# A graph kernel on one core: the mask product of its one-hot gather in float32r instead of bf16

## The chip, the cores and the metric

The kernel runs on one core of one Trainium2 chip. The metric is the device time of one execution in microseconds (us). TensorE is the matrix engine, with weight loads and matmuls as instructions of their own; VectorE, ScalarE and GpSimd are the other engines, and the queue that starts plain transfers is called SP. In the profile they are PE and PEld (the loads), DVE, ACT, POOL and SP.

## The reference

There are 12500 nodes with 16 features and 412500 edges, sorted by their destination. Three edge-conditioned convolutions are followed by a layer that takes a maximum over edges.

```python
def _nnconv(x, src, dst, edge_attr, ew, eb, rw, rb):
    W = (edge_attr @ ew + eb).reshape(edge_attr.shape[0], x.shape[1], rw.shape[1])
    xj = x[src]
    msg = jnp.einsum('ei,eio->eo', xj, W)
    agg = jax.ops.segment_sum(msg, dst, num_segments=x.shape[0])
    return agg + x @ rw + rb
...
# the last layer
msg = inputs[src] * timestamp
h = jax.ops.segment_max(msg, dst, num_segments=inputs.shape[0])
return h @ W.T + b
```

Each of the four layers therefore needs the rows `x[src]` of all its edges: a gather of 412500 rows.

## The kernel before

**The chunks.** The edges lie as 128 streams, one on each partition, and a stream is cut into 124 chunks of 26 edges. `edges` (L556) runs over the chunks in each of the four layers, two chunks in a loop body, with two buffers of everything (slots 0 and 1). Of a chunk's 26 columns, 16 (`TG`) are fetched by GpSimd with one indirect DMA each (`pool_gather`, L461), from a table in memory. The other 10 (`TP`) are gathered by TensorE.

**TensorE's gather.** One step (`pe_step`, L619) fetches 128 rows. A node number is split in three: a lane (128), a zone (4) and a block in the zone (25, `NEAR`). The stationary operand `hot_key` is a one-hot matrix of the lanes, one for each zone; the moving operand is one zone of the node table, 25 blocks of 16 features, so 400 columns. The table is held in two float32r parts that add up to the float32 value, so 4 zones times 2 parts make eight products, accumulated in one PSUM bank. They leave the features of all 25 blocks. A ninth product, over 25 rows, adds to every block but the right one a large negative number: `not_near` is a huge number times the distance of the edge's block number from each of the 25, and `near_mask` is minus the unit matrix, each entry repeated 16 times. VectorE then takes the maximum over the 25 blocks (`pick`, L741), which gives the 16 features. There are four such banks; a step waits until the pick of four steps earlier has freed its bank (`s_pick`), and a pick waits for the ninth product (`s_gath`). Products take one weight load and one matmul each.

**ScalarE** makes the one-hot matrices out of keys that SP loads: `apart` (L508), `hot_key` (L513) and, last for a chunk, `not_near` (L524), each of 1280 columns for a chunk's 10 steps.

**The order in a chunk.** TensorE's order is written out in `pe_body` (L657): steps 4 to 6 of a chunk, a transpose of the first five picked rows (`pe_turn`, L637), steps 7 and 8, the product of those with the edge weights (`pe_product`, L649), step 9, then steps 0 to 3 (`HEAD`) of the following chunk with the second transpose and product among them. VectorE's order in `body` (L747) is: picks 4 and 5 of the next chunk; the product of the gathered rows with the edge attributes; pick 6; the same product for TensorE's rows; pick 7; the sum over features (L804); pick 8; the indices for the chunk after the next (L845), on which GpSimd waits; the second sum; pick 9; then picks 0 to 3 of the chunk after that, with 16 scans (L828) between them. In the max layer there are no transposes and no products by TensorE, and the indices follow pick 6.

**Start and layers.** All inputs are loaded once by SP, `near_mask` among them (L203); `vector_masks` (L247) prepares masks and keys on VectorE before the first layer. `parts_of_h` (L881 to 883) writes the table's two parts before each layer. Between layers lie batch norms, small products and a gather of each node's last edge.

Of the kernel before, what the change touches and what calls it, by code (L numbers as in the profile page):

```python
# [5 lines left out]
F32, BF16, F16, I32 = mybir.dt.float32, mybir.dt.bfloat16, mybir.dt.float16, mybir.dt.int32  # L6
F32R = mybir.dt.float32r
# [5 lines left out]
N, D, EF, E, LAYERS = 12500, 16, 8, 412500, 3  # L13
# [18 lines left out]
NEAR = 25  # L32
# [4 lines left out]
PE_EDGES = TP * P  # L37
# [14 lines left out]
def build(nc, io):  # L52
    ctx = ExitStack()

    def sb(name, shape, dt=F32):
        return ctx.enter_context(nc.sbuf_tensor(name, shape, dt))
# [4 lines left out]
    def slots(make, name, *a):  # L61
        return [make(f"{name}{s}", *a) for s in range(SLOTS)]

    with ctx:
# [37 lines left out]
        edge_i = sb("edge_i", [P, 4], I32)  # L102
# [19 lines left out]

        parts = [sb(f"part{k}", [P, ZONES * NEAR, D], F32R) for k in range(2)]
        zone_lane = sb("zone_lane", [P, ZONES + 1])
        near_mask = sb("near_mask", [NEAR, NEAR, D], BF16)
        keys = slots(sb, "keys", [P, PE_EDGES], F16)
        nears = slots(sb, "nears", [P, PE_EDGES], F16)
        apart = slots(sb, "apart", [P, PE_EDGES], F16)
        hot_key = slots(sb, "hot_key", [P, ZONES, PE_EDGES], F32R)
        not_near = slots(sb, "not_near", [NEAR, PE_EDGES], BF16)  # L130
        xe = slots(sb, "xe", [P, TP * D])
        xeT = sb("xeT", [TH * D, P])

# [60 lines left out]
        def bump(s, n=1):  # L194
# [5 lines left out]
                       (ident, io["ident"]), (conv_w, io["conv_w"][0])]  # L200
        loads = [(pe_src, io["pe_src"]), (src, io["src"]), (lanes, io["lanes"]),
                 (real, io["real"]), (lin_w, io["lin_w"]), (gamma, io["gamma"]), (beta, io["beta"]),
                 (edge_i, io["borders"]), (zone_lane, io["zone_lane"]), (near_mask, io["near_mask"]),  # L203
                 (row_i, io["borders_row"]), (edge_w, io["edge_w"][0])]

        def sync_start(e):
# [8 lines left out]
        def step(e, ins):  # L215

            ins.then_inc(s_step.sem, 1)
            s_step.n += 1
            e.wait_ge(s_step.sem, s_step.n)

        def tt(e, out, a, b, op):
            return e.tensor_tensor(out, a, b, op)  # L222
# [23 lines left out]

        def vector_masks(e):  # L247
            e.wait_ge(s_in.sem, IN_ALL)
            first, last, prev_last, next_first = (edge_i[:, k:k + 1] for k in range(4))
            tt(e, edge_m[:, 0:1], first, prev_last, ALU.is_equal)  # L250
            tt(e, edge_m[:, 1:2], first, last, ALU.is_equal)
            step(e, tt(e, edge_m[:, 2:3], next_first, last, ALU.is_equal))

            step(e, tt(e, edge_m[:, 3:4], edge_m[:, 1:2], edge_m[:, 2:3], ALU.mult))
            step(e, e.tensor_scalar(edge_m[:, 4:5], edge_m[:, 3:4], -1.0, 1.0, ALU.mult, ALU.add))
            e.tensor_scalar(head_lo_i[:, 0:1], first, P - 1, None, ALU.bitwise_and)
            step(e, e.tensor_scalar(head_lo_i[:, 1:2], first, 7, None, ALU.logical_shift_right))
            step(e, e.tensor_copy(edge_m[:, 0:2], head_lo_i[:, 0:2]))
            step(e, e.tensor_scalar(head_lo[:, :], lanes[:, :], edge_m[:, 0:1], edge_m[:, 4:5],
                                    ALU.is_equal, ALU.mult))  # L260
            step(e, e.tensor_scalar(head_hi[:, :], lanes[:, 0:NB], edge_m[:, 1:2], None, ALU.is_equal))

            rf, rpl, rpf = (row_i[:, k, :] for k in range(3))
            tt(e, row_m[:, 0, :], rf, rpl, ALU.is_equal)
            step(e, tt(e, row_m[:, 1, :], rpf, rpl, ALU.is_equal))
            step(e, tt(e, row_m[:, 2, :], row_m[:, 0, :], row_m[:, 1, :], ALU.mult))

            e.tensor_scalar(row_m[:, 3, :], row_m[:, 0, :], BIG, -BIG, ALU.mult, ALU.add)
            step(e, e.tensor_scalar(row_m[:, 4, :], row_m[:, 2, :], BIG, -BIG, ALU.mult, ALU.add))

            step(e, e.tensor_scalar(zone_f, pe_src, float(NEAR * P), None, ALU.is_ge))
            for z in range(2, ZONES):
                step(e, e.scalar_tensor_tensor(zone_f, pe_src, float(z * NEAR * P), zone_f, ALU.is_ge, ALU.add))

            step(e, e.scalar_tensor_tensor(pe_tmp, zone_f, -float(NEAR * P), pe_src, ALU.mult, ALU.add))
            step(e, e.tensor_scalar(pe_tmp, pe_tmp, 7, None, ALU.logical_shift_right))
            step(e, e.tensor_copy(keys[1][0:CHUNKS, :], pe_tmp))

            step(e, e.tensor_scalar(pe_src, pe_src, P - 1, None, ALU.bitwise_and))
            e.scalar_tensor_tensor(keys[0][0:CHUNKS, :], zone_f, float(P), pe_src, ALU.mult,  # L280
                                   ALU.add).then_inc(s_v.sem, 1)
# [3 lines left out]
        def masks_and_keys():  # L285

            on("vector")(vector_masks)
            v = bump(s_v)

            def sync_keys(e):  # L290
                e.wait_ge(s_v.sem, v)
                for ap, half in ((key_rows, keys[0]), (near_rows, keys[1])):
                    e.dma_start(ap, half[0:CHUNKS, :]).then_inc(s_keys.sem, 16)
                e.wait_ge(s_keys.sem, 32)
            on("sync")(sync_keys)
# [1001 lines left out]
```

## Time and profile before

| what | us |
|---|---|
| median of 3 runs | 17138.0 (17130.03 to 17155.55) |
| the profiled execution, its own time | 17104.02 |
| span in its profile | 17102.1 |
| TensorE matmuls busy | 12418.0 |
| GpSimd busy | 8073.4 |
| VectorE busy | 7231.8 |
| ScalarE busy | 6262.2 |

The span runs from the first to the last instruction. The mean granted clock of TensorE was 0.81 of its full 2.4 GHz; it is granted at full or at half. The first three layers take the most time; the last begins after about 13000 us. Busy times are sums over stretches of very different kinds, and a matmul's end is modelled by the profiler, so a busy TensorE need not be the bound.

### The profile page before, as it was taken

What the parts mean: (1) busy time and instruction counts of PE and PEld (TensorE: products, weight loads), DVE (VectorE), ACT (ScalarE), POOL (GpSimd) and SP (SyncE); (2) the same over time, 40 slices, a digit from 0 to 9 for tenths busy, and PEclk for the clock granted to TensorE, in tenths of its full rate; (3) what the DMA queues carried; (4) which work ended last, traced back from release to release, by engine and by line L of the source; (5) the groups of instructions that cost most, each with busy time, mean ns of one, the idle gap of its engine ahead of it and who ended that gap; (6) DMA issues with size and microseconds to landing.
All of it is one profiled execution on the core that took longest, in us unless ns stands there. A gap on an engine that the chain in (4) does not pass through costs nothing.

```text
span 17102.1 us, 173153 instructions
## 1 busy us (share of the span) xinstructions
PE 12418.0 (73%) x48794; PEld 8988.7 (53%) x48794; DVE 7231.8 (42%) x15692; ACT 6262.2 (37%) x6911; POOL 8073.4 (47%) x8528
## 2 busy tenths in 40 slices
PE   4777777777277777777747777777775777777774
PEld 2555555555155555555535555555553555555553
DVE  3444444444344444444434444444443333333232
ACT  2333333333133333333323333433332333333332
POOL 4444444444544444444444444444445455555555
PEclk7888888888688888888878888888887888888887
DMA  2222222222122222222212222222221111111111
GB/s 64 58 57 57 58 57 57 58 58 58 41 56 57 57 57 57 58 57 58 58 41 64 57 58 58 58 57 58 57 57 40 24 26 25 26 25 26 25 26 18
DMA packets 555882, 838.15 MB, mean 49 GB/s; under 512 B 192965, under 2 KB 381695, under 8 KB 555590
## 3 DMA queue, kind: packets, MB, share of 16 engines
q0 software_dynamic: 272768, 465.16, 13.0%
q1 hardware_dynamic: 283078, 372.58, 7.2%
q8 instruction: 14, 0.23, 0.0%
q14 instruction: 22, 0.18, 0.0%
HBM read 707.52 MB, written 129.56 MB: 49 GB/s over the span
## 4 chain that ended last, share of the span: by engine, by line
PE 49%; another core or an unknown queue 24%; issue 18%; ACT 3%; DVE 3%; POOL 1%; DMA 1%; ACTq 0%; DVEq 0%; SPq 0%; POOLq 0%
PE pY L627 37%; PE pY L629 6%; PE pY L649 5%; ACT hot_key L513 2%; DVE run L828 1%; ACT not_near L524 1%; POOL gathered L461 1%; PE pT L637 1%; DVE xe L741 1%; ACT apart L508 1%; DMA edge_w<-in_edge_w 0%; DMA conv_table<-rows 0%; ACTq L190 0%; ACT xeT L699 0%
## 5 line engine op out<-in xcount | busy, mean ns | idle before, releaser
L627 PE MATMUL pY<-part,hot_key 128*128 128x400 f32 x39680 | 10168.6, 395 | 2810.9 <-issue 2336.7
L627 PEld LDWEIGHTS pY<-part,hot_key 128*128 128x128 f32 x39680 | 7924.0, 213 | 4093.0 <-issue 3395.6
L461 POOL DMA_INDIRECT gathered<-conv_table,idx x5952 | 5630.6, 946 | 6852.3 <-DVE idx L845 4888.3
L741 DVE TENSOR_REDUCE xe<-pY 128x16 f32<-128x400 f32 x4960 | 2749.1, 571 | 9048.1 <-remote 4952.2
L508 ACT ACTIVATE apart<-keys,zone_lane 128x1280 f16<-128x1280 f16 x1984 | 2595.9, 1358 | 2739.1 <-PE pY L629 1700.9
L710 ACT COPY gathered<-pY 128x432 f32<-128x432 f32 x1488 | 610.8, 462 | 6497.7 <-remote 5433.5
L461 POOL DMA_INDIRECT gathered<-max_table,idx x1984 | 1878.2, 947 | 1802.1 <-DVE idx L845 1152.8
L513 ACT ACTIVATE hot_key<-apart 128x1280 fp32r<-128x1280 f16 x1984 | 2401.5, 1260 | 0.0
L629 PE MATMUL pY<-near_mask,not_near 25*128 25x400 bf16 x4960 | 1820.9, 367 | 309.9 <-issue 309.3
L804 DVE TENSOR_REDUCE msg<-gathered 128x256 f32<-128x2304 f32 x744 | 1558.6, 2095 | 0.2
L828 DVE TENSOR_TENSOR_SCAN run<-same,run,msg 128x26 f32<-128x26 f32 x7936 | 1477.5, 260 | 0.6
L222 DVE TENSOR_TENSOR gathered<-gathered,attr 128x2048 f32<-128x2048 f32 x744 | 1399.9, 1882 | 0.1
L629 PEld LDWEIGHTS pY<-near_mask,not_near 25*128 25x128 bf16 x4960 | 457.7, 92 | 1785.0 <-issue 1785.0
L649 PE MATMUL pY<-edge_w,xeT 80*128 80x432 f32 (+1 forms) x2976 | 1101.2, 493 | 71.6 <-ACT xeT L699 60.5
L649 PEld LDWEIGHTS pY<-edge_w,xeT 80*128 80x128 f32 x2976 | 505.0, 189 | 473.5 <-issue 432.4
L637 PE MATMUL pT<-ident,xe 128*80 128x128 f32 x744 | 273.5, 368 | 583.5 <-DVE xe L741 577.0
L524 ACT ACTIVATE not_near<-nears,zone_lane 25x1280 bf16<-25x1280 f16 x496 | 667.0, 1345 | 0.0
L637 PEld LDWEIGHTS pT<-ident,xe 128*80 128x80 f32 x744 | 95.7, 129 | 782.8 <-DVE xe L741 641.3
L461 POOL DMA_INDIRECT gathered<-scanned,idx x392 | 374.0, 954 | 208.4 <-issue 123.7
L699 ACT COPY xeT<-pT 80x128 f32<-80x128 f32 x744 | 183.9, 247 | 611.6 <-PE pT L637 342.6
L392 PE MATMUL pT<-ident,hs 128*113 128x128 f32 x70 | 28.8, 426 | 448.5 <-ACT hs L367 327.0
L392 PEld LDWEIGHTS pT<-ident,hs 128*113 128x113 f32 x70 | 16.7, 245 | 455.3 <-ACT hs L367 254.8
(112 smaller groups left out, 933.6 us busy)
## 6 DMA issues: line engine op xcount, KB each, us to landing
keys<-key_rows SPq DMA_DIRECT2D x496, 320.0 KB
scanned<-run SPq DMA_DIRECT2D x496, 208.0 KB
gathered<-conv_table,idx POOLq DMA_INDIRECT x5952
attr<-in_attr SPq DMA_DIRECT2D x372, 104.0 KB
gathered<-max_table,idx POOLq DMA_INDIRECT x1984
nears<-near_rows SPq DMA_DIRECT2D x496, 62.5 KB
conv_table<-rows SPq DMA_DIRECT2D x42, 504.0 KB, 3.3
gathered<-scanned,idx POOLq DMA_INDIRECT x392
```

What stands on the lines that cost most here:

```text
L222: return e.tensor_tensor(out, a, b, op)
L461: e.indirect_dma_start(out=G[s][:, t, 0:width], out_offset=None, in_=table[:, :], in_offset=bass.IndirectOffsetOnAxis(ap=idx[s][:, t:t + 1 ...
L508: e.activation(apart[k][:, :], keys[s][:, :], ACT.Abs, bias=zone_lane[:, z:z + 1]).then_inc(s_abs.sem, 1)
L513: e.activation(hot_key[s][:, z, :], apart[k][:, :], ACT.Relu, bias=1.0, scale=-1.0).then_inc(s_abs.sem, 1)
L524: e.activation(not_near[s][:, :], nears[s][0:NEAR, :], ACT.Abs, bias=zone_lane[0:NEAR, ZONES:ZONES + 1], scale=FAR).then_inc(s_hotk[s].sem, 1)
L627: e.matmul(pG[bank], hot_key[s][:, z, j * P:(j + 1) * P], part[:, z * NEAR:(z + 1) * NEAR, :], start=(z == 0 and k == 0), stop=False)
L629: e.matmul(pG[bank], not_near[s][:, j * P:(j + 1) * P], near_mask[:, :, :], start=False, stop=True).then_inc(s_gath.sem, 1)
L649: ins = e.matmul(pE[:, q, 0:m * ROW], xeT[:, :], edge_w[:, k * ROW:(k + m) * ROW], start=True, stop=True)
L710: ins = e.copy(G[s][:, TG + half * TH + k:TG + half * TH + k + m, :], pE[:, q, 0:m * ROW].rearrange("p (t c) -> p t c", c=ROW))
L741: e.tensor_reduce(xe[s][:, j * D:(j + 1) * D], pG[g % BANKS].rearrange("p (r d) -> p d r", d=D), AX.X, ALU.max).then_inc(s_pick.sem, 1)
L804: return mark(e.tensor_reduce(msg[:, a:b, :].rearrange("p t d -> p (t d)"), g[:, a:b, :].rearrange("p t (d f) -> p (t d) f", f=FB), AX.X, ...
L828: ins = e.tensor_tensor_scan(run[s][:, :, d], flags, msg[:, :, d], run[1 - s][:, T - 1, d:d + 1], ALU.add if is_max else ALU.mult, ALU.max ...
```

## The change

The ninth product's two operands become float32r, the type of the eight others. The mask tile is no longer loaded at its full width but as a 25 x 25 matrix, in a tile of its own, and VectorE spreads it over the 16 features once at the start, which also makes it float32r. Nothing else moves: the number and order of TensorE's instructions, the waits and the shapes of operands stay as they are.

```diff
--- before.py
+++ after.py
@@ -122,12 +122,13 @@
 
         parts = [sb(f"part{k}", [P, ZONES * NEAR, D], F32R) for k in range(2)]
         zone_lane = sb("zone_lane", [P, ZONES + 1])
-        near_mask = sb("near_mask", [NEAR, NEAR, D], BF16)
+        near_mask = sb("near_mask", [NEAR, NEAR, D], F32R)
+        near_in = sb("near_in", [NEAR, NEAR])
         keys = slots(sb, "keys", [P, PE_EDGES], F16)
         nears = slots(sb, "nears", [P, PE_EDGES], F16)
         apart = slots(sb, "apart", [P, PE_EDGES], F16)
         hot_key = slots(sb, "hot_key", [P, ZONES, PE_EDGES], F32R)
-        not_near = slots(sb, "not_near", [NEAR, PE_EDGES], BF16)
+        not_near = slots(sb, "not_near", [NEAR, PE_EDGES], F32R)
         xe = slots(sb, "xe", [P, TP * D])
         xeT = sb("xeT", [TH * D, P])
 
@@ -200,7 +201,7 @@
                        (ident, io["ident"]), (conv_w, io["conv_w"][0])]
         loads = [(pe_src, io["pe_src"]), (src, io["src"]), (lanes, io["lanes"]),
                  (real, io["real"]), (lin_w, io["lin_w"]), (gamma, io["gamma"]), (beta, io["beta"]),
-                 (edge_i, io["borders"]), (zone_lane, io["zone_lane"]), (near_mask, io["near_mask"]),
+                 (edge_i, io["borders"]), (zone_lane, io["zone_lane"]), (near_in, io["near_mask"]),
                  (row_i, io["borders_row"]), (edge_w, io["edge_w"][0])]
 
         def sync_start(e):
@@ -246,6 +247,7 @@
 
         def vector_masks(e):
             e.wait_ge(s_in.sem, IN_ALL)
+            e.tensor_copy(near_mask[:, :, :], near_in[:, :].unsqueeze(2).to_broadcast([NEAR, NEAR, D]))
             first, last, prev_last, next_first = (edge_i[:, k:k + 1] for k in range(4))
             tt(e, edge_m[:, 0:1], first, prev_last, ALU.is_equal)
             tt(e, edge_m[:, 1:2], first, last, ALU.is_equal)
@@ -1274,7 +1276,7 @@
         "edge_w": np.stack(edge_w),
         "zone_lane": -np.concatenate([order[:, None] + P * np.arange(ZONES), FAR * order[:, None]], axis=1
                                      ).astype(np.float32),
-        "near_mask": -np.eye(NEAR, dtype=np.float32).astype(mybir.dt.np(BF16))[:, :, None].repeat(D, 2),
+        "near_mask": -np.eye(NEAR, dtype=np.float32),
 
         "pe_src": streams(f["src"], 0).reshape(P, CHUNKS, T)[:, :, TG:].transpose(1, 2, 0).reshape(
             CHUNKS, PE_EDGES),
```

## Rows read from the trace of the kernel before

**Rows 1.** the page: span, busy time, share and instructions of each engine

```profile
span 17102.1 us, 173153 instructions
...
PE 12418.0 (73%) x48794; PEld 8988.7 (53%) x48794; DVE 7231.8 (42%) x15692; ACT 6262.2 (37%) x6911; POOL 8073.4 (47%) x8528
```

**Rows 2.** VectorE's timeline, a convolution's chunk: start us, us, what, idle before

```profile
3096.07 0.17 DVE L845 TENSOR_SCALAR idx<-src 128x16 int32 x1
...
3114.87 0.58 DVE L741 TENSOR_REDUCE xe<-pY 128x16 f32<-128x400 f32 x1 [11.34 <-PE pY L629]
3119.81 1.54 DVE L741 TENSOR_REDUCE xe<-pY 128x16 f32<-128x400 f32 x3 [4.36 <-remote]
...
3128.77 0.17 DVE L845 TENSOR_SCALAR idx<-src 128x16 int32 x1
```

**Rows 3.** GpSimd's timeline, that chunk's 16 gathers: first, second, last

```profile
3097.04 0.94 POOL L461 DMA_INDIRECT gathered<-conv_table,idx  x1 [13.68 <-DVE idx L845]
3098.28 0.94 POOL L461 DMA_INDIRECT gathered<-conv_table,idx  x1 [0.30 <-issue]
...
3115.77 0.94 POOL L461 DMA_INDIRECT gathered<-conv_table,idx  x1 [0.30 <-issue]
```

**Rows 4.** TensorE's timeline, matmuls of that chunk

```profile
3101.44 0.31 PE L637 MATMUL pT<-ident,xe 128*80 128x128 f32 x1
3101.50 1.70 PE L627 MATMUL pY<-part,hot_key 128*128 128x400 f32 x8
3103.13 0.34 PE L629 MATMUL pY<-near_mask,not_near 25*128 25x400 bf16 x1
...
3105.06 0.34 PE L629 MATMUL pY<-near_mask,not_near 25*128 25x400 bf16 x1
```

**Rows 5.** groups by line: busy us, mean ns, idle before and its enders

```profile
L627 PEld LDWEIGHTS pY<-part,hot_key 128*128 128x128 f32 x39680 | 7924.0, 213 | 4093.0 <-issue 3395.6 <-DVE xe L741 584.2 <-DVE part L883 16.4
...
L741 DVE TENSOR_REDUCE xe<-pY 128x16 f32<-128x400 f32 x4960 | 2749.1, 571 | 9048.1 <-remote 4952.2 <-PE pY L629 3130.3 <-issue 960.8
...
L513 ACT ACTIVATE hot_key<-apart 128x1280 fp32r<-128x1280 f16 x1984 | 2401.5, 1260 | 0.0
...
L524 ACT ACTIVATE not_near<-nears,zone_lane 25x1280 bf16<-25x1280 f16 x496 | 667.0, 1345 | 0.0
...
L629 PEld LDWEIGHTS pY<-near_mask,not_near 25*128 25x128 bf16 x4960 | 457.7, 92 | 1785.0 <-issue 1785.0
...
L881 DVE CAST part<-h 128x1568 fp32r<-128x1568 f32 x4 | 3.9, 972 | 0.2
```

**Rows 6.** a stretch's length, then busy PE, PEld, DVE, ACT, POOL

```profile
3119.50:3129.70 10.20, 9.95 (x34) 7.39 (x34) 9.89 (x11) 7.82 (x10) 0.00 (x0) 0.69 0.11 36
```

**Rows 7.** VectorE's timeline, a chunk of the max layer

```profile
14073.13 0.57 DVE L741 TENSOR_REDUCE xe<-pY 128x16 f32<-128x400 f32 x1 [12.12 <-remote]
...
14080.08 0.57 DVE L741 TENSOR_REDUCE xe<-pY 128x16 f32<-128x400 f32 x1 [1.89 <-PE pY L629]
...
14080.80 0.17 DVE L845 TENSOR_SCALAR idx<-src 128x16 int32 x1
```

**Rows 8.** TensorE's timeline, matmuls of that chunk of the max layer

```profile
14060.59 0.34 PE L629 MATMUL pY<-near_mask,not_near 25*128 25x400 bf16 x1
...
14073.76 3.04 PE L627 MATMUL pY<-part,hot_key 128*128 128x400 f32 x8 [7.05 <-issue]
...
14077.17 2.60 PE L627 MATMUL pY<-part,hot_key 128*128 128x400 f32 x8
```

**Rows 9.** GpSimd's timeline, that chunk's first gather

```profile
14052.54 0.94 POOL L461 DMA_INDIRECT gathered<-max_table,idx  x1 [9.41 <-DVE idx L845]
```

**Rows 10.** timelines of short stretches: two matmuls, three, a load at half clock

```profile
3030.73 0.53 PE L627 MATMUL pY<-part,hot_key 128*128 128x400 f32 x2
...
3030.73 0.71 PE L627 MATMUL pY<-part,hot_key 128*128 128x400 f32 x3
...
3058.86 0.33 PEld L627 LDWEIGHTS pY<-part,hot_key 128*128 128x128 f32 x1
```

## Prediction

> **What bounds the kernel now.** I read the page first. No engine is full: TensorE's matmuls are busy 12418 of 17102 us, GpSimd 8073, VectorE 7232, ScalarE 6262 [rows 1]. So shares decide nothing, and I went to the timeline of one chunk in a convolution, then in the max layer, asking what ends each wait.
>
> Every chunk has the same turn. VectorE writes the indices of a later chunk (L845), GpSimd starts 0.97 us later and issues 16 gathers at 1.25 us each, 3097.04 to 3115.77 plus 0.94, so 19.67 us [rows 2, 3]. While it does, VectorE's picks (L741) stop being told of finished steps. The reader is to see that the mask product of 3103.13 has run, with its 0.34 us, by 3103.47 [rows 4], yet VectorE's next pick starts at 3114.87 after 11.34 us idle, and the three behind it only at 3119.81, all at once, 3.1 us after the last gather was issued [rows 2, 3]. TensorE's increments arrive late, and the profile cannot name the releaser: 4952 us of the picks' idle time stand as "remote" [rows 5]. I call this the freeze. When it ends VectorE works without a hole, 9.89 busy of 10.20 us, to the next indices at 3128.77 [rows 2, 6]. The turn closes: 0.97 + 19.67 + 3.10 + 8.96 = 32.70 us. There are 3 x 124 chunks of this kind. TensorE stands on this path only through how many picks are left to do when the freeze ends.
>
> In the max layer the turn is shorter and its last part is TensorE's. The mask product of 14060.59 is picked at 14073.13, after 12.12 us; VectorE frees a PSUM bank, TensorE, which had all four full and sat 7.05 us, starts at 14073.76 and needs two more steps, at half clock at first, before the pick of 14080.08, for which VectorE waited 1.89 us on the mask product; the indices follow at 14080.80 [rows 7, 8]. One batch started at 14052.54 [rows 9]; the next starts 0.95 us after those indices, 29.2 us later. There are 124 such chunks.
>
> **The change, part by part.** *The step on TensorE.* A step is eight float32r products and one bf16 one, on 25 rows. Products of one kind follow each other at 0.18 us at full clock (0.71 less 0.53) and 0.33 at half clock, where the weight loads, 0.33 long, follow without a gap [rows 10]. A whole step takes 3105.06 - 3103.13 = 1.93 us [rows 4] and at half clock 14077.17 - 14073.76 = 3.41 [rows 8]. Nine at the common spacing would be 1.62 and 3.0. So the odd one costs 0.3 (0.4 at half clock) beyond its own share: its load starts with it, not under the one before, and the next step's loads are late too. The load is no prefetch there (1785 us idle before 4960 such loads, 0.36 each, [rows 5]). The trace does show that a change of operand alone need not cost this: the float32 transpose at 3101.44, on 128 rows, is followed by a float32r product 0.06 us later [rows 4]. No row has a four-byte product on 25 rows amid the stream. Bounds: nothing saved, its load growing from 92 ns to the 213 of L627's [rows 5], so 0.12 us a step lost; or all 0.3 saved. I take all of it, since the row nearest in type, the transpose, is joined to its neighbours. Over 4960 steps that is 1.4 ms of TensorE's time, most of it in the shade of the freeze.
>
> One page speaks against the change. The Trainium skill, TensorE: Matmul & The Clock Gate, Weight-path perf modes, has a fast weight load for all types but FP32; the trace agrees that the bf16 load is the shorter, 92 against 213 ns [rows 5]. By that page alone the change lengthens the load and a step grows by about 0.1 us; by the spacing it shrinks by 0.3.
>
> *In the convolutions.* After the freeze VectorE is the bound, so a faster step gives nothing there. Before it, between indices and freeze, TensorE does about four steps and gains 4 x 0.3 = 1.2 us on the start of the freeze, which goes by the gathers as far as these two turns tell. The product that just missed (ending 6.4 us into the batch at 3097.04) would end at 5.2. If its increment gets through, one pick of 0.48 us (1.54 us for three, overlapped) is off the path. Bounds 0 and 0.48 us a chunk; in the turn shown one pick got through alone anyway, so I take half, 0.25: 372 x 0.25 = 93 us.
>
> *In the max layer.* Two steps on the path save 0.4 + 0.3 = 0.7 us: 124 x 0.7 = 87 us. Beyond it, the missed product ended 8.4 us into its batch; with five steps since the indices it would end at 6.9, maybe in time. Each time it is, four banks further along are full at the end of the freeze and one step less, 3.0 less the 0.4 counted, stands behind it. Bounds 0 and 2.6 us; since the increment must beat a freeze that began by 6.4 in the convolution, I take a quarter, 0.6: 74 us.
>
> *ScalarE.* The mask activation (L524) has 1280 columns at 1345 ns and writes bf16; L513 writes float32r of 1280 columns in 1260 [rows 5]. Between 0.1 less and nothing; it lies in ScalarE's idle time (6262 busy us in all), and if that cover went it would be 496 x 0.1 = 50 us at most. Zero. *Start.* One VectorE copy of 400 elements replaces most of a load, and float32r copies of 1568 take 972 ns (L881, [rows 5]): under 1 us once. Zero.
>
> Sum: 93 + 87 + 74 = 254 us. Against the profiled execution's own 17104.0 us (span 17102.1) that is 16850; the median of the runs shown is 17138, 34 us higher, so 16884, rounded to 16880 us.
>
> **The rivals.** (1) *The row count, not the type, breaks the stream.* Then the step stays near 1.93 us, and its load may grow by 0.12. For it: no row separates the two causes. The Trainium skill, TensorEngine Tiling (Array Packing), Key Properties, says that a change of tiling mode drains TensorE; if 25 rows make such a mode the odd product keeps its cost. With nothing else changed the time is 17138. (2) *The same, and the longer load is paid, on both clocks:* the side of slower. On the path it counts twice in a max chunk and perhaps once in a convolution's: 124 x 0.24 + 372 x 0.12 = 75 us, so 17210. It decides once more than 34 us stay exposed, some 0.05 us a step. (3) *The step is faster but the freeze follows TensorE's own work, not the gathers.* Then no increment comes sooner: only the 87 us of the max layer count, 17050. For it: both freezes begin where four banks later TensorE is blocked anyway; against it: the beginning lies 6.4 and 8.4 us after the first gather, in layers with different work. (4) *Every missed increment gets through:* 372 x 0.48 + 87 + 124 x 2.6 = 588 us, so 16550.
>
> **How the numbers follow.** Forecast, partly through: 0.42. Rival 3: 0.20. Rival 1: 0.14. Rival 2: 0.13. Rival 4: 0.11. A measurement of this kernel tells 0.2%, 34 us, from no change. Faster sums the forecast, rivals 3 and 4, less some for a gain that is given back at another wait: 0.68; same 0.17; slower 0.15. The range reaches from rival 4's side, 16580, past no change to 17170, and leaves out most of rival 2 and half of rival 4. The faster cases alone lie within 16550 to 17060.
>
> **What would show it.** The step: L629's weight load under the matmul before it, no idle before it, and steps of 1.62 us at full clock. The max layer: chunks of some 28 us instead of 29.2 and a shorter wait before the pick that precedes the indices. The convolutions: chunks of 32.4 instead of 32.7, and fewer picks run together at the end of the freeze. If L629's load still starts with its matmul, rival 1 or 2 holds. If the step is 1.62 and the convolution's chunks stay at 32.7, rival 3. The sum goes most wrong if the freeze itself moves or lengthens, which no row lets me price.

## The result and the profile after: the wrong sign, by 520 us

The changed kernel takes 17662.37 us (median of 4 runs, 17647.23 to 17706.53), the kernel before 17142.57 beside it. The ratio is 1.0307, with a 95% interval of 1.0287 to 1.0328: slower by 520 us, where 16880 was predicted and 17170 was the top of the range.

The page of the changed kernel (span, busy time, and TensorE's granted clock in 40 slices, in tenths of full speed):

```profile
span 17650.6 us, 173154 instructions
...
PE 13717.6 (78%) x48794; PEld 10153.5 (58%) x48794; DVE 7275.9 (41%) x15693; ACT 6256.3 (35%) x6911; POOL 8066.7 (46%) x8528
...
PEclk7888888888688888888878888888886676767676
```

TensorE's matmuls, equally many, are busy 1300 us more than in [rows 1]; all other engines do the same work. The clock row falls from 8 to 6 and 7 in the last quarter, the max layer. All lines have moved by two: L627 is L629 now, the mask product L631, the pick L743, the indices L847, the gathers L463.

The changed kernel's groups of the mask product, matmul and load, that answer to [rows 5] (busy us, mean ns, idle before and what ended it):

```profile
L631 PE MATMUL pY<-near_mask,not_near 25*128 25x400 f32 x4960 | 2511.7, 506 | 239.4 <-issue 239.2
...
L631 PEld LDWEIGHTS pY<-near_mask,not_near 25*128 25x128 f32 x4960 | 1037.2, 209 | 1845.4 <-issue 1845.4
```

The mask product's load has grown from 92 to 209 ns and has the same idle time ahead of it as before, 1845 against 1785 us. So it is still no prefetch. TensorE's own timelines of a step at full clock show this more closely; first the matmuls, then the loads of the changed kernel:

```profile
3047.51 0.45 PE L631 MATMUL pY<-near_mask,not_near 25*128 25x400 f32 x1
3047.88 1.72 PE L629 MATMUL pY<-part,hot_key 128*128 128x400 f32 x8
3049.53 0.45 PE L631 MATMUL pY<-near_mask,not_near 25*128 25x400 f32 x1
```

```profile
3047.51 0.18 PEld L631 LDWEIGHTS pY<-near_mask,not_near 25*128 25x128 f32 x1 [0.26 <-issue]
3047.88 1.39 PEld L629 LDWEIGHTS pY<-part,hot_key 128*128 128x128 f32 x8 [0.19 <-issue]
```

The load of 3047.51 begins with its matmul, after 0.26 us in which the loads stood still, and the next step's first load waits until 3047.88. The kernel before, at full clock, in the chunk of [rows 8]:

```profile
14079.70 0.34 PE L629 MATMUL pY<-near_mask,not_near 25*128 25x400 bf16 x1
14079.97 1.72 PE L627 MATMUL pY<-part,hot_key 128*128 128x400 f32 x8
```

From the mask product to the next step's first product it is 0.37 us now (3047.51 to 3047.88) and was 0.27 (14079.70 to 14079.97). The step is 2.02 to 2.03 us against 1.93 [rows 4].

**By layer.** Each mask product stands for one step, so their number in equal stretches is the pace. A stretch of 3600 us in the first convolution and one of 3000 in the max layer, kernel before, the mask product alone (length, busy, count, clock, DMA):

```profile
400.00:4000.00 3600.00, 403.73 (x1090) 0.82 0.23 57
...
13800.00:16800.00 3000.00, 367.04 (x1021) 0.84 0.13 26
```

and the changed kernel, all four layers:

```profile
400.00:4000.00 3600.00, 524.28 (x1075) 0.82 0.22 57
5000.00:8600.00 3600.00, 516.34 (x1063) 0.81 0.22 56
9400.00:13000.00 3600.00, 522.22 (x1066) 0.81 0.22 56
13800.00:16800.00 3000.00, 529.52 (x942) 0.70 0.12 24
```

A layer has 1240 steps. The first takes 3600 x 1240 / 1075 = 4153 us against 4095, 57 more; the others 100 and 92 more (1089 and 1090 steps before), and the max layer 3000 x 1240 / 942 = 3949 against 3643, 306 more. Together 555 us, about the 548 between the two spans. Taken whole, from its first mask product to its last, the first layer is 67 us longer, the next two 98 and 83, and the max layer 302 (3951 against 3649), so the stretches stand for their layers. Per chunk that is 0.67 us in a convolution and 2.5 in the max layer.

**What a slower max chunk looks like.** TensorE's matmuls, then VectorE, in the changed kernel's max layer:

```profile
14520.21 3.04 PE L629 MATMUL pY<-part,hot_key 128*128 128x400 f32 x8
14523.17 0.70 PE L631 MATMUL pY<-near_mask,not_near 25*128 25x400 f32 x1
...
14526.77 0.70 PE L631 MATMUL pY<-near_mask,not_near 25*128 25x400 f32 x1
14527.40 1.82 PE L629 MATMUL pY<-part,hot_key 128*128 128x400 f32 x8
```

```profile
14520.32 0.57 DVE L743 TENSOR_REDUCE xe<-pY 128x16 f32<-128x400 f32 x1 [3.02 <-PE pY L631]
...
14523.91 0.57 DVE L743 TENSOR_REDUCE xe<-pY 128x16 f32<-128x400 f32 x1 [2.69 <-PE pY L631]
...
14524.63 0.17 DVE L847 TENSOR_SCALAR idx<-src 128x16 int32 x1
...
14557.01 0.17 DVE L847 TENSOR_SCALAR idx<-src 128x16 int32 x1
```

Steps are 3.60 us long (14523.17 to 14526.77), at half clock, where those of [rows 8] were 3.41. All steps from 14480.68 to 14527.40 are so, thirteen in a row without a gap and at a granted clock of 0.50, then the clock goes up. In the chunk of [rows 8] it was up within the second step. It isn't one chunk alone: of the max layer's 1239 spacings between mask products, 499 are the 3.59 us of half clock, up to fourteen in a row, where in the kernel before 36 are its 3.41 us and no two follow each other. VectorE waits about 3 us for the picks before the indices, TensorE is now the bound there, and from indices to indices it is 32.4 us. The slice of [rows 7 to 9] took 29.2.

### The profile page after: what moved, and what is told of

It reads as the page before. It is cut to its first block, busy times and chain, and to the rows that moved or that the text cites. A ratio compares the mean times of both kernels' runs of the same rounds, so it can differ in the third digit from the quotient of the medians.

```text
span 17650.6 us, 173154 instructions
## 1 busy us (share of the span) xinstructions
PE 13717.6 (78%) x48794; PEld 10153.5 (58%) x48794; DVE 7275.9 (41%) x15693; ACT 6256.3 (35%) x6911; POOL 8066.7 (46%) x8528
## 4 chain that ended last, share of the span: by engine, by line
PE 68%; issue 15%; another core or an unknown queue 12%; DVE 3%; POOL 1%; ACT 1%; DMA 1%; ACTq 0%; DVEq 0%; SPq 0%; POOLq 0%
PE pY L629 49%; PE pY L631 11%; PE pY L651 6%; PE pT L639 1%; DVE run L830 1%; POOL gathered L463 1%; DVE xe L743 1%; ACT hot_key L515 0%; DMA edge_w<-in_edge_w 0%; DMA conv_table<-rows 0%; ACT not_near L526 0%; PE pY L405 0%; DMA conv_w<-in_conv_w 0%; ACT apart L510 0%
## 5 line engine op out<-in xcount | busy, mean ns | idle before, releaser
L629 PE MATMUL pY<-part,hot_key 128*128 128x400 f32 x39680 | 10689.6, 413 | 2066.4 <-issue 1771.4
L629 PEld LDWEIGHTS pY<-part,hot_key 128*128 128x128 f32 x39680 | 8456.2, 226 | 3291.7 <-issue 2782.2
L463 POOL DMA_INDIRECT gathered<-conv_table,idx x5952 | 5626.7, 945 | 7103.9 <-DVE idx L847 5140.4
L743 DVE TENSOR_REDUCE xe<-pY 128x16 f32<-128x400 f32 x4960 | 2754.1, 571 | 9553.9 <-remote 4347.7
L463 POOL DMA_INDIRECT gathered<-max_table,idx x1984 | 1874.6, 945 | 2106.5 <-DVE idx L847 1458.8
L631 PE MATMUL pY<-near_mask,not_near 25*128 25x400 f32 x4960 | 2511.7, 506 | 239.4 <-issue 239.2
L631 PEld LDWEIGHTS pY<-near_mask,not_near 25*128 25x128 f32 x4960 | 1037.2, 209 | 1845.4 <-issue 1845.4
L651 PE MATMUL pY<-edge_w,xeT 80*128 80x432 f32 (+1 forms) x2976 | 1243.5, 545 | 271.6 <-issue 257.2
L651 PEld LDWEIGHTS pY<-edge_w,xeT 80*128 80x128 f32 x2976 | 558.8, 209 | 738.1 <-issue 724.6
L526 ACT ACTIVATE not_near<-nears,zone_lane 25x1280 fp32r<-25x1280 f16 x496 | 667.8, 1346 | 0.0
L463 POOL DMA_INDIRECT gathered<-scanned,idx x392 | 374.0, 954 | 208.6 <-issue 123.6
```

Source lines behind the costliest of these rows:

```text
L463: e.indirect_dma_start(out=G[s][:, t, 0:width], out_offset=None, in_=table[:, :], in_offset=bass.IndirectOffsetOnAxis(ap=idx[s][:, t:t + 1 ...
L526: e.activation(not_near[s][:, :], nears[s][0:NEAR, :], ACT.Abs, bias=zone_lane[0:NEAR, ZONES:ZONES + 1], scale=FAR).then_inc(s_hotk[s].sem, 1)
L629: e.matmul(pG[bank], hot_key[s][:, z, j * P:(j + 1) * P], part[:, z * NEAR:(z + 1) * NEAR, :], start=(z == 0 and k == 0), stop=False)
L631: e.matmul(pG[bank], not_near[s][:, j * P:(j + 1) * P], near_mask[:, :, :], start=False, stop=True).then_inc(s_gath.sem, 1)
L651: ins = e.matmul(pE[:, q, 0:m * ROW], xeT[:, :], edge_w[:, k * ROW:(k + m) * ROW], start=True, stop=True)
L743: e.tensor_reduce(xe[s][:, j * D:(j + 1) * D], pG[g % BANKS].rearrange("p (r d) -> p d r", d=D), AX.X, ALU.max).then_inc(s_pick.sem, 1)
```

## The experiments

The kernel before did not take the same time on each occasion: 17141.31 us beside one group of experiments and 16879.04 beside another, but 11797.98, 11778.11 and 11779.97 beside the other three. In the traces of the first two occasions the freeze of the prediction is there, in those of the other three it is not; it is not tied to a chip, since one chip showed 17141 and 11778. Of the kernel before there is no trace from the occasion of 16879, so what set it 262 us below 17141 stays open. Each number below is therefore a ratio to the kernel before, run among them on the same occasion, with its 95% interval, and the text says "with the freeze" or "without".

### What keeps the product out of the stream: type or rows

*f32r_128, f32r_64* (without the freeze; line numbers move by two to four): the changed kernel with 128 or 64 rows in the mask product's operands, rows 25 and up being zeros in `near_mask`, so that they add nothing; *bf16_128*: the same for the kernel before.

```diff
+MASK_ROWS = 128
...
-        near_mask = sb("near_mask", [NEAR, NEAR, D], F32R)
+        near_mask = sb("near_mask", [MASK_ROWS, NEAR, D], F32R)
...
-        not_near = slots(sb, "not_near", [NEAR, PE_EDGES], F32R)
+        not_near = slots(sb, "not_near", [MASK_ROWS, PE_EDGES], F32R)
...
+                e.memset(nears[s][:, :], 0.0)
...
-            e.activation(not_near[s][:, :], nears[s][0:NEAR, :], ACT.Abs,
+            e.activation(not_near[s][:, :], nears[s][0:MASK_ROWS, :], ACT.Abs,
...
-        "near_mask": -np.eye(NEAR, dtype=np.float32),
+        "near_mask": -np.eye(MASK_ROWS, NEAR, dtype=np.float32),
```

> The changed kernel with its mask product over 128 partitions instead of 25 (the rows from 25 on are zero in the mask tile). Theory A, the row count breaks the stream: the mask product's load runs under the matmul before it, the step falls from 2.03 to 9 x 0.18 = 1.65 us at full clock and from 3.59 to 3.0 at half clock, and the time falls below that of the kernel before, to about 16600 to 16900 us. Theory B, something else about the ninth product (the last of its group, or the other operand tile) breaks it: the step stays at 2.03 us and the time at 17660.

> The kernel before with its bf16 mask product over 128 partitions instead of 25. If the row count alone breaks the stream, the step falls from 1.93 to about 1.6 us and the time below that of before, as in the float32r kernel on 128 rows. If a change of operand type breaks it as well, the step stays at 1.93 us and the time at 17140.

> The changed kernel with its mask product over 64 partitions. If only a product on the full height is joined, the step stays at 2.03 us and the time at 17660; if the break is one between 32 rows and more, the step is 1.65 us and the time that of 128 rows.

Measured: f32r_128 11788.81 us, ratio 0.9992 (0.9982 to 1.0001); bf16_128 11790.63, 0.9993 (0.9984 to 1.0003); f32r_64 12109.42, 1.0265 (1.0248 to 1.0282). Then again with the freeze, where there is something to gain, and with 96 rows (*f32r_96*):

> The changed kernel with its mask product over 128 partitions, again, for a chip on which the kernel before takes 17140 us; on the chip of its first run, where before took 11798 us, its step was 1.63 us and its time 0.9992 of before. Theory A (a shorter step lets one more pick through before the freeze and shortens the tail of the max layer): 16550 to 16900 us. Theory B (the freeze takes back what TensorE gains): within 0.3% of before. With no freeze on this chip: 11790 us again.

> The kernel before with its bf16 mask product over 128 partitions, again, likewise; its step was 1.61 us on the chip of 11798 us. Theory A: 16550 to 16900 us, within 0.5% of the float32r kernel on 128 rows, so that the type costs nothing once the product is joined. Theory B: within 0.3% of before. With no freeze: 11790 us.

> The changed kernel with its mask product over 96 partitions. On 64 the step was 2.03 us, on 128 1.63, and the products over 80 rows by line 651 are joined to their neighbours. If more than 64 rows are enough, the step is 1.63 us and the time that of 128 rows; if the product must be as high as its neighbours, 2.03 us and the time of the changed kernel.

Measured: f32r_128_b 16696.94, 0.9886 (0.9870 to 0.9903); bf16_128_b 16707.44, 0.9892 (0.9876 to 0.9909); f32r_96 16695.25, 0.9890 (0.9874 to 0.9907). TensorE's matmuls and loads in f32r_128_b:

```profile
3047.36 0.34 PE L633 MATMUL pY<-near_mask,not_near 128*128 128x400 f32 x1
3047.54 1.62 PE L631 MATMUL pY<-part,hot_key 128*128 128x400 f32 x8
3048.99 0.34 PE L633 MATMUL pY<-near_mask,not_near 128*128 128x400 f32 x1
```

```profile
3047.18 0.19 PEld L633 LDWEIGHTS pY<-near_mask,not_near 128*128 128x128 f32 x1
3047.36 1.46 PEld L631 LDWEIGHTS pY<-part,hot_key 128*128 128x128 f32 x8
```

Here the load stands ahead of its matmul, with no idle time on either side, and a step is 3048.99 - 3047.36 = 1.63 us. In bf16_128 it is 1.65 (2049.46 to 2051.11), and not the 1.61 that I wrote under bf16_128_b; with 96 rows it is 1.63 (2012.58 to 2014.21, f32r_96_b). With 64 rows nothing has changed against 25, as TensorE's timeline of f32r_64 shows:

```profile
2048.39 0.45 PE L633 MATMUL pY<-near_mask,not_near 64*128 64x400 f32 x1
2048.77 1.48 PE L653 MATMUL pY<-edge_w,xeT 80*128 80x432 f32 x4
```

It is 0.38 us from the mask product to what follows it. The edge product itself, with 80 rows, is joined to the stream. Its loads and the next step's, in f32r_128_b:

```profile
3054.00 0.37 PEld L653 LDWEIGHTS pY<-edge_w,xeT 80*128 80x128 f32 x2
...
3055.15 1.52 PEld L631 LDWEIGHTS pY<-part,hot_key 128*128 128x128 f32 x8
```

The first load stands under the mask product of that time (3054.00 to 3054.34), its matmul follows at 3054.18, and the next step's loads start at 3055.15, before the last of the four edge matmuls is over (3055.55). So 25 and 64 rows break the stream and 80, 96 and 128 do not; at 25 and at 128 rows this is so with either type, the other heights were run in float32r or float32 alone. The Trainium skill, TensorEngine Tiling (Array Packing), lists modes of 32 and 64 rows under Tiling Modes and says under Key Properties that a change of mode drains TensorE. The five heights agree with that; the drain itself is no row of a trace.

### Is it the longer load, or anything longer

*bf16_extra*: the kernel before with a second mask product of 16 columns, so the step ends with two short ones. *bf16_wide*: the same with 256 columns.

```diff
                 e.matmul(pG[bank], not_near[s][:, j * P:(j + 1) * P], near_mask[:, :, :],
+                         start=False, stop=False)
+                e.matmul(pG[bank][:, 0:D], not_near[s][:, j * P:(j + 1) * P], near_mask[:, 0, :],
                          start=False, stop=True).then_inc(s_gath.sem, 1)
```

> The kernel before with a second bf16 product of 16 columns after the mask product, over the same 25 rows (it adds the mask of the first block once more), to make a step longer without float32r. Theory A, the length of the step is all that costs: with a step of about 2.05 us the time comes out at 17600 to 17750 us, with TensorE at half clock through whole chunks of the max layer as in the changed kernel. Theory B, the float32r product itself keeps the clock low or lengthens the freeze: the time stays below 17300 us and the max layer's clock at about 0.8.

> The kernel before with the second small bf16 product, again, likewise; it makes a step 2.0 us long with bf16 operands. With the freeze: theory A, the length of the step is what costs, gives about 17500 us (two thirds of the changed kernel's 520 us) and a lower clock in the max layer; theory B, the float32r product over few rows is what keeps the clock low, gives under 17300 us and a max layer clock of 0.8. With no freeze: 11800 us again.

> The kernel before with a second bf16 mask product, of 256 columns instead of 16 (it adds the mask of 16 of the 25 blocks once more). The small one of 16 columns made a step only 0.01 us longer; 240 columns more add 0.1 us at full clock and 0.2 at half, so the step is that of the changed kernel, 2.04 and 3.62 us, with bf16 operands. On a chip with the freeze: if the length of the step keeps TensorE at half clock through whole chunks of the max layer, its granted clock there falls from 0.83 to about 0.71 and the layer grows by 200 to 300 us over the kernel with 16 columns; if float32r over 25 rows is what does it, the clock stays at 0.83 and the layer grows by under 100 us. With no freeze: 12110 us, the time of the float32r kernel on 64 rows.

> The kernel before with the second bf16 mask product of 256 columns, again, for a chip with the freeze; its step is 2.03 us. There: about 300 us over the kernel with 16 columns, which took 1.015 of before. The max layer's clock falls to 0.71 if a longer step is enough for that, and stays at 0.83 if not. With no freeze: 3.0% over before again.

Measured: bf16_extra, without the freeze, 11803.52, 1.0004 (0.9994 to 1.0014); bf16_extra_b, with it, 17138.51, 1.0151 (1.0134 to 1.0168). The small product lengthens the step hardly, to 1.95 us (3048.47 to 3050.42), so the pair does not decide between the two theories, and the 259 us that it costs with the freeze are more than the 99 that 0.02 us come to over 4960 steps; what it is, the runs leave open (below). bf16_wide, without the freeze, 12132.05, 1.0301 (1.0283 to 1.0318), and bf16_wide_b 12130.91, 1.0299 (1.0283 to 1.0315). TensorE in bf16_wide_b:

```profile
2002.58 0.34 PE L629 MATMUL pY<-near_mask,not_near 25*128 25x400 bf16 x1
2002.76 0.27 PE L631 MATMUL pY<-near_mask,not_near 25*128 25x256 bf16 x1
2002.96 1.73 PE L627 MATMUL pY<-part,hot_key 128*128 128x400 f32 x8
2004.62 0.34 PE L629 MATMUL pY<-near_mask,not_near 25*128 25x400 bf16 x1
```

A bf16 step of 2.04 us costs 3.0%, a float32r step of 2.03 us costs 2.7% (next). Without the freeze these two are told apart by the step's length and not by the type. Both runs were meant for the freeze and met none, so whether a longer bf16 step also keeps the clock of the max layer low there is not tested.

### The changed kernel without the freeze

*after_again* is the changed kernel as it is; *f32r_96_b* is f32r_96 once more. Both without the freeze.

> The changed kernel, unchanged, so that the two others have it on their own chip. With the freeze: 3.0 to 3.3% over before. With no freeze it has not been run: the float32r kernel on 64 rows, whose step is the same, was 2.65% over before there, all of it in the convolutions, so 12110 us.

> The changed kernel with the mask product over 96 partitions, again. With no freeze: GpSimd's gathers bound every chunk, so within 0.2% of before, as with 128 rows (0.9992). With the freeze: 1.1% faster than before again.

Measured: after_again 12097.5, 1.0270 (1.0253 to 1.0287), or 319 us; f32r_96_b 11769.49, 0.9992 (0.9983 to 1.0001). The stretch in the convolutions and one in the max layer, after_again, all engines (length, busy PE, PEld, DVE, ACT, POOL, clock, DMA); then the first of these for f32r_96_b:

```profile
400.00:2900.00 2500.00, 2500.00 (x10974) 1899.27 (x10973) 1747.67 (x3406) 1421.23 (x1647) 1899.51 (x1758) 1.00 0.33 83
9500.00:11800.00 2300.00, 2299.78 (x10214) 1781.22 (x10213) 1038.76 (x3280) 1248.28 (x1020) 1721.91 (x1807) 1.00 0.18 37
```

```profile
400.00:2900.00 2500.00, 2275.18 (x11414) 2119.59 (x11413) 1783.11 (x3541) 1480.28 (x1707) 1913.89 (x1827) 0.97 0.33 86
```

TensorE is busy all 2500 us in after_again, and its mask products set the pace below: it is the bound, at full clock. With 96 rows it has 225 us to spare, and the pace is GpSimd's: a chunk takes 21.9 us (2500 / 114.1), of which 16 gathers at 1.25 are 20.0. The mask products alone say what each makes of the same time, after_again and then f32r_96_b:

```profile
400.00:2900.00 2500.00, 488.86 (x1098) 1.00 0.33 83
```

```profile
400.00:2900.00 2500.00, 406.07 (x1141) 0.97 0.33 86
```

3 x 1240 x (2500 / 1098 - 2500 / 1141) = 319 us: the whole cost lies in the convolutions, 0.86 us a chunk, and the max layer, at full clock here, costs nothing. The two engines are nearly even in a convolution: in bf16_extra TensorE was busy 2497.74 of the 2500 us and still kept GpSimd's pace, 1140 steps. That is why, without the freeze, a longer step costs so much there and a shorter one gives nothing.

### Whose work the freeze puts on the path

*before_here* and *after_here* are the two kernels as they are; *before_17* and *after_17* issue a 17th gather per chunk, into a tile that nothing reads.

```diff
+                        if steps == TG:
+                            e.indirect_dma_start(
+                                out=spare[:, s, 0:width], out_offset=None, in_=table[:, :],
+                                in_offset=bass.IndirectOffsetOnAxis(ap=idx[s][:, 0:1], axis=0)
+                            ).then_inc(got[s].sem, 16)
...
-                gate(e, "dve", got[s], i * (16 * TG) + 16 * TG)
+                gate(e, "dve", got[s], i * (16 * (TG + 1)) + 16 * (TG + 1))
```

> The kernel before, unchanged, for its profile beside the last runs, in which it took 11798 us instead of 17143. Theory A, those runs have no freeze: picks follow their mask product by 0.04 us all through, GpSimd's gathers of one chunk follow those of the last without a wait for indices, and a convolution's chunk takes about 21.9 us, both GpSimd's 16 gathers and TensorE's 10 steps. If the freeze comes back on this chip, the time is about 17140 us and the picks wait 10 us and more during the gathers.

> The changed kernel, unchanged. Theory A, where there is no freeze a convolution's chunk is bound by TensorE once its step grows from 1.93 to 2.03 us: 10 x 0.1 = 1.0 us less what GpSimd's bound hid, so 0.85 us in each of 372 chunks, and nothing in the max layer, where GpSimd's gathers take 20.0 us and the ten steps 20.3: 12110 us, 2.6% over before. Theory B, the price is in the freeze and in the half clock: then here it costs under 1%. With the freeze: 17660 us again.

> The kernel before with one more gather by GpSimd in each chunk of the four layers, into a tile that nobody reads. Theory A (no freeze): GpSimd's 17 gathers bound every chunk, 1.3 us more each, so about 11800 + 496 x 1.3 = 12440 us. Theory B (TensorE alone sets the chunks): under 11900 us.

> The changed kernel with the same added gather. Theory A (no freeze): GpSimd is the bound in both, and the change costs nothing beside the kernel before with 17 gathers: within 0.3% of it, where it costs 2.6% with 16. If the longer mask load cost time in any other way than by the bound that TensorE sets, the same 300 us would stand between the two with 17 gathers as well.

Measured, all with the freeze: before_here 17144.75, 1.0000 (0.9991 to 1.0009); after_here 17700.48, 1.0323 (1.0309 to 1.0337); before_17 17696.13, 1.0326 (1.0310 to 1.0342); after_17 17961.64, 1.0477 (1.0461 to 1.0493). The 17th gather costs 17696 - 17141 = 555 us over 496 chunks, 1.12 us each, nearly the 1.25 of its spacing [rows 3]: GpSimd's batch is on the path, as the prediction had it. In the changed kernel it costs only 261, and the change costs 265 with it where it costs 559 without. Where the rest goes is seen by layer, from the first to the last mask product of each (us):

| | three convolutions | max layer |
|---|---|---|
| before_here | 12298 | 3659 |
| after_here | 12583 | 3958 |
| before_17 | 12709 | 3807 |
| after_17 | 12795 | 4001 |

The change costs 285 us in the convolutions and 299 in the max layer; with the 17th gather it is 86 and 194. So a longer batch gives TensorE most of the time for its longer steps in the convolutions, and only a third of it in the max layer, where the granted clock of after_17 is 0.72 against 0.82 in before_17 (13800 to 16800 us).

Where a chunk of a convolution loses its time with the freeze is in the same traces. Between the first pick after the batch and the next indices VectorE takes 10.4 us on the mean in after_here and 9.7 in before_here, and 0.5 us of those 0.7 are longer idle time (1.14 against 0.60). So TensorE is on that part of the path too.

### What keeps the clock low

*f32r_seven* and *bf16_seven* leave out the product of the last zone's low part, so seven products and the mask product: a shorter step, with everything else of the changed kernel or of the one before.

```diff
-                    for k, part in enumerate(parts):
+                    for k, part in enumerate(parts[:1 if z == ZONES - 1 else 2]):
```

> The changed kernel without one of its eight one-hot products (the low part of the last zone is left out), float32r mask on 25 rows: the step falls by one spacing, to 1.85 us at full clock and 3.26 at half, under that of the kernel before. If the length of the step decides, the max layer is back at a clock of about 0.83 and the time at or under that of before. If the float32r product on few rows keeps the clock low, the layer still has whole chunks at half clock (0.71). With no freeze: 11790 us.

> The kernel before without one of its eight one-hot products (the low part of the last zone is left out), with its bf16 mask product: the step is 1.75 us at full clock and 3.08 at half. The changed kernel with the same product left out (step 1.85 and 3.26 us) sat at half clock through the whole max layer, 1500 us longer than before's. Theory A, the float32r operands of the short product do that: here the max layer is at a clock of 0.8 or more and takes 2520 us. Theory B, it is the make of the step (less matmul in it beside the breaks), whatever the type: here too whole chunks of the max layer pass at half clock, at 30.8 us a chunk, and the layer takes up to 3800 us.

Measured, both without the freeze but on two occasions: f32r_seven 13322.66, 1.1309 (1.1290 to 1.1327); bf16_seven 11786.78, 1.0004 (0.9995 to 1.0014). The first is the great surprise of these runs: its step at full clock is 1.85 us, less than that of the kernel before, and its convolutions keep nearly the pace (1133 steps in the 2500 us, bf16_seven 1140). Its max layer, then that of bf16_seven (all engines, as above):

```profile
9500.00:11800.00 2300.00, 2300.00 (x5645) 1717.13 (x5644) 648.12 (x2040) 774.04 (x633) 1068.03 (x1125) 0.50 0.11 23
```

```profile
9500.00:11800.00 2300.00, 1958.40 (x8334) 1456.12 (x8333) 936.45 (x3074) 1136.16 (x963) 1688.22 (x1768) 0.89 0.17 34
```

f32r_seven has no idle time on TensorE in these 2300 us and is granted 0.50 throughout. So it is from the first to the last mask product of the layer, which takes 4039 us (9136 to 13175) where that of bf16_seven takes 2516: the 1523 us between them are about all of the 13%. TensorE in it, and then in bf16_seven after a wait:

```profile
9500.64 0.70 PE L631 MATMUL pY<-near_mask,not_near 25*128 25x400 f32 x1
9501.26 2.70 PE L629 MATMUL pY<-part,hot_key 128*128 128x400 f32 x7
```

```profile
9509.72 2.60 PE L627 MATMUL pY<-part,hot_key 128*128 128x400 f32 x7 [1.23 <-DVE xe L741]
9512.25 0.51 PE L629 MATMUL pY<-near_mask,not_near 25*128 25x400 bf16 x1
9512.69 1.79 PE L627 MATMUL pY<-part,hot_key 128*128 128x400 f32 x7
```

With the bf16 mask product TensorE is at half clock after a wait of 1.23 us and back within the next step; the longest stretch in that layer is three steps (10144.69 to 10153.91). With the float32r one on 25 rows the step is 3.26 us at half clock (9500.64 to 9503.90), and at half clock it stays, with no wait for VectorE in it. In the changed kernel it does come back, but after up to fourteen steps. None of the rows that I had read showed such a stretch: in [rows 8] the clock is back within the second step. A longer step isn't needed for it, since the one of f32r_seven is shorter than the one of the kernel before at either clock, 1.85 against 1.93 us and 3.26 against 3.41. Whether the type does it or the longer stop around its load isn't settled: at half clock the stop is 0.62 us with the one (9500.64 to 9501.26) and 0.44 with the other (9512.25 to 9512.69).

## Why the prediction was wrong, by its own steps

**The failed step.** "I take all of it, since the row nearest in type, the transpose, is joined to its neighbours." The transpose has the type of the stream and 128 rows, so it had no say on which of the two joins it. I wrote under rival 1 that no row separates the causes, yet took the whole gain and gave rivals 1 and 2 together 0.27. The edge product was the row to weigh: 80 rows and joined, while the mask product had 25. Neither row tells 25 rows of float32r, so a half share for the bound of nothing saved was the honest reading. The runs show the product on 25 rows outside the stream with either type, and in it on 96 and 128 rows: the step went from 1.93 to 2.03 us and not to 1.62. The bound itself, "its load growing from 92 ns to the 213 of L627's, so 0.12 us a step lost", is what came: 209 ns and 0.10 us.

**Rival 2 held, at seven times its price.** It had the right mechanism, "the same, and the longer load is paid, on both clocks", and 75 us for it, 124 x 0.24 + 372 x 0.12. The convolutions measured 0.67 us a chunk instead of 0.12, 250 us in all, and the max layer 2.5 instead of 0.24, 306 us. In the convolutions the 0.12 counted one step on the path. With the freeze most of the loss is VectorE's longer wait for TensorE between the freeze and the indices, 0.5 us a chunk; without it, where TensorE is nearly even with GpSimd, all ten steps of a chunk count, 0.86 us for 10 x 0.10. In the max layer I took the share of steps at half clock as fixed by the kernel before. It was not: the clock of that stretch fell from 0.84 to 0.70, and 499 spacings instead of 36 are those of half clock. Each of them is 1.57 us longer than one at full clock (3.59 against 2.02), where I had priced each of two steps of a chunk at 0.12. With the clock at 1.00, in after_again, the same longer step costs nothing in that layer.

**The downstream price, given a joined step, was too high by 72 us.** Predicted: 93 + 87 + 74 = 254 us. A joined step was had with 96 or 128 rows and gave 16879 - 16697 = 182 us with the freeze. I had allowed for the freeze hiding most of 1.4 ms: it does, 182 us are left of 4960 x 0.3. The split over convolutions and max layer was not measured, since there is no trace of the kernel before from that occasion, so whether 93, 87 and 74 were each near is not shown.

**Rival 3** (the freeze follows TensorE's own work) isn't what the runs show of its end: a 17th gather makes the kernel before slower by 1.12 us a chunk and moves the first pick after the batch from 23.8 to 25.2 us behind the indices (medians of the first convolution's chunks, before_here and before_17), and in the changed kernel that time is the same as in [rows 2], 23.7 us (3119.81 - 3096.07). VectorE of the changed kernel, a chunk of a convolution:

```profile
3046.16 0.16 DVE L847 TENSOR_SCALAR idx<-src 128x16 int32 x1
...
3067.70 0.57 DVE L743 TENSOR_REDUCE xe<-pY 128x16 f32<-128x400 f32 x1 [13.69 <-remote]
3069.88 1.55 DVE L743 TENSOR_REDUCE xe<-pY 128x16 f32<-128x400 f32 x3 [1.61 <-remote]
...
3076.30 0.57 DVE L743 TENSOR_REDUCE xe<-pY 128x16 f32<-128x400 f32 x1 [0.78 <-PE pY L631]
...
3079.73 0.16 DVE L847 TENSOR_SCALAR idx<-src 128x16 int32 x1
```

The three picks at the end of the freeze start 3069.88 - 3046.16 = 23.7 us after the indices. What follows isn't without a hole any more: VectorE waits 0.78 us at 3076.30 for a mask product, and the indices are at 9.85 us instead of 8.96, so 33.6 us a chunk and not 32.7. I had written that "a faster step gives nothing there"; a slower one has a price, and the faster one was not measured there on the same occasion as the kernel before. Of the beginning of the freeze the traces say more for rival 3 than I gave it. In the max layer of before_here the first step to be picked over 5 us late is the same one of a chunk's ten in 74 of 88 chunks, and its mask product ends 7.9 us into the batch (median). In f32r_128_b, on another occasion, it ends at 7.0 and is still the one that is late in 78 of 92. In the convolutions it is 6.4 us, and then 5.8, the same step in 286 of 346 chunks and then in 185 of 353. So finishing sooner got an increment through in part of the convolutions' chunks and hardly ever in the max layer; the beginning is not a fixed time after the first gather. What does set it was not tried alone. **Rival 4** needed the faster step, and with it the gain was 182 us, not 588.

**ScalarE and the start.** ScalarE's activation went from 1345 to 1346 ns, inside its idle time, and the start's copy leaves no trace in the time: both zeros held. The page on the weight path that I cited (the Trainium skill, TensorE: Matmul & The Clock Gate, Weight-path perf modes) gave the sign, and I let the spacing outweigh it.

## What to carry to other kernels

Before a short product is costed as "one more of the stream", look for a row of the same height as well as of the same type: here 25 and 64 rows cost two stops in every step and zero rows up to 96 took them away, for 1.1% less time than the kernel before where the freeze was there, and none less where it wasn't. Put a range on both sides of a step that is nearly even with another engine's: 0.1 us longer cost 2.7 to 3.2%, 0.3 us shorter gave 1.1% at most. And when a change lengthens steps in a stretch where the clock goes up and down, its share at half clock is not a constant.

## What the runs showed of the hardware that I had not expected

**Late increments, on some occasions.** One program took 17141 us and 11778 us on the same chip. What differs is the freeze, during which TensorE itself only creeps. TensorE in the changed kernel while GpSimd issues the batch that began at 3047.13:

```profile
3062.72 0.49 PE L629 MATMUL pY<-part,hot_key 128*128 128x400 f32 x1 [2.26 <-issue]
3064.16 0.49 PE L629 MATMUL pY<-part,hot_key 128*128 128x400 f32 x1 [0.95 <-issue]
3065.57 0.68 PE L629 MATMUL pY<-part,hot_key 128*128 128x400 f32 x1 [0.92 <-issue]
3067.68 0.49 PE L631 MATMUL pY<-near_mask,not_near 25*128 25x400 f32 x1 [1.43 <-issue]
```

Its products come 1.4 to 2.1 us apart and wait for nothing that the profile shows, and those of the stream are joined again at 3069.81, when the batch is over. That a load and a matmul of 16 columns, 0.02 us of step, cost 1.5% with the freeze and nothing without would fit a price per instruction in this time; I did not measure it, and what turns the freeze on is open.

**A clock that stays down.** Seven products and a float32r mask product on 25 rows held TensorE at half clock through the whole max layer, 4039 us, without idle time in the 2300 us shown (0.50), while the same with bf16 was granted 0.89 and rose within a step in the chunk shown. With the mask product on 96 or 128 rows, of either type that was run, no trace has more than two steps in a row at half-clock spacing.
